# A graph layer on one core: node bias read from row 0 of the message buffers, y sums for a pair at once, second block scaled on VectorE

## The chip, the cores and the metric

The kernel runs on one core of a Trainium2 chip. A core has TensorE (PE in the profile, with its weight loads as PEld), VectorE (DVE), ScalarE (ACT), GpSimd (POOL), a queue engine SyncE (SP) and 16 DMA engines that all queues share. The metric is device time in microseconds (us), as a median of several runs.

## What is computed

The graph has 50,000 nodes and 25,000 edges sorted by `dst`, with rows of 128 numbers. Each edge's message is a normalised, gated product of its two end rows; messages with the same `dst` are averaged; each node is then updated from its own row and its mean message, and the result is normalised.

```python
em = jnp.concatenate([x[src], x[dst]], axis=-1)
em = jax.nn.relu(layer_norm(em @ msg_w + msg_b, msg_g, msg_beta)) * edge_weights[:, None]
msgs = jax.ops.segment_sum(em, dst, num_segments=num_nodes)
messages = msgs / (counts + 1e-08) * valid
gate = jax.nn.sigmoid(x @ gate_w + gate_b)
h_new = jax.nn.relu(layer_norm(jnp.concatenate([x, messages], -1) @ upd_w + upd_b, upd_g, upd_beta))
out = layernorm(x + gate * h_new + (1.0 - gate) * x)
```

## The kernel before, in words

Edges go in 49 groups of 512 (4 tiles of 128), nodes in 98 blocks of 512, two blocks to a pair, so 49 pairs. One step of the main loop handles one edge group and the parts of one pair, at different depths of the pipeline. Each engine has its own `step` function that lists its tasks by hand with a lag (how many steps the pair is behind the edge group) and a block number, 0 or 1. That list is the whole order; there is no scheduler. `walk` runs the steps, the middle ones in a loop.

An edge group: GpSimd gathers 8 tiles of rows of `x` (L466). PE transposes them, multiplies by the message weights into `ps_z` (L727, L729), on top of a bias matmul (L703). ACT squares, DVE scales (L1019), PE transposes back and multiplies (L742), DVE writes `msg_rows` (L1026), and SP stores them to the scratch table `rows_scratch` (L403). A row there is 129 numbers, 516 bytes: 128 values and the node's number.

A block of nodes: SP loads its `x_rows` (L366) and a **window** of the scratch table that holds all messages of the block: four tiles of 128 rows of 129, two to a DMA, the second DMA shifted by 64 rows (`load_window`, L384). The start row comes from a table, so each window DMA has its place in a register. DVE turns the node numbers in the window into a selection matrix `onehot` (`one_hots`, L1034). PE adds three products into `ps_u`: the bias (L703, bf16, one for two tiles), the node's own row (L761) and the selected messages (L763). ACT takes squares (L555), 1/deviation (L576, L581) and scales to `un` (L588), for both blocks. PE transposes (L778), ACT applies relu (L601), PE transposes back (L785), DVE forms `y` (L1048), its statistics (L1055), small sums of 4 numbers a partition (L1065 to L1085), ACT two small functions (L606, L611), DVE the output (L1100), and SP stores it (L399).

There are four window buffers, so SP may load a pair's two windows once the pair two before is through its updates (`pair_ready`); it must also wait until the next edge group's rows have landed in the scratch table (L376, L379), for the windows read them. All of SP's DMAs go through one queue, q1.

Of the kernel before, what the change touches and what calls it, by code (L numbers as in the profile page):

```python
# [6 lines left out]
ALU = mybir.AluOpType  # L7
# [13 lines left out]
FAR = float(1 << 20)  # L21
LN_EXP_SET = 6
# [28 lines left out]
def const_columns(wt):  # L51

    sizes = [P, T * P, 2 * T * P, 2 * T, 2, wt, 3, 1, T]
    return [sum(sizes[:i]) for i in range(len(sizes) + 1)]


def gnn_kernel(nc, x, src, dst, edge_weight, msg_w, msg_b, msg_g, msg_beta,  # L60
# [17 lines left out]
    C_IDENT, C_IOTA, C_BOUND, C_BOUNDC, C_TBASE, C_TILE, C_PART, C_LIMIT, C_WIN, C_END = const_columns(WT)  # L78

    with ExitStack() as ctx:  # L80
# [16 lines left out]
        iota_block = const_in[:, C_IOTA:C_IOTA + BN]  # L97
        tile_base = const_in[:, C_TILE:C_TILE + WT]
# [6 lines left out]
        msg_bias, upd_bias = sb("msg_bias", [P, T, P], BF16), sb("upd_bias", [P, 2, ROW], BF16)  # L105
        columns = sb("columns", [P, 4])
        gather_idx = sb("gather_idx", [P, EG, 2 * T], I32)
# [25 lines left out]
        gate_exp = [sb(f"gate_exp{s}", [P, T]) for s in range(2)]  # L133
        gate_small = [sb(f"gate_small{s}", [P, 3, T]) for s in range(2)]
        un = [sb(f"un{s}", [P, 512]) for s in range(2)]
        hT = [sb(f"hT{s}", [P, 512]) for s in range(2)]
        y = [sb(f"y{s}", [P, 512]) for s in range(2)]
        y_stats = [sb(f"y_stats{s}", [P, T, 6]) for s in range(2)]
        y_small = [sb(f"y_small{s}", [P, 6, T]) for s in range(2)]
        y_ln = [sb(f"y_ln{s}", [P, T]) for s in range(2)]  # L140
        y_rstd = [sb(f"y_rstd{s}", [P, T]) for s in range(2)]
# [23 lines left out]
        def u_tile(j, n):  # L165
# [3 lines left out]
            "p a (t h) -> p a t h", h=ROW)  # L169
        u_gates = u_by_bank[:, :, :, P:ROW]  # L170
# [3 lines left out]
        bias_in = sb("bias_in", [P, 2, ROW])  # L174
        bias_mean = sb("bias_mean", [P, 2])
        bias_left = sb("bias_left", [P, 3, 2, ROW])
        bias_part = sb("bias_part", [P, 3, 2, ROW], BF16)
        bias_sum = sb("bias_sum", [P, 3, 2, ROW])
# [109 lines left out]

        def all_edges(eng, task):
# [28 lines left out]
        def _(sp):  # L318
# [52 lines left out]
            def pair_ready(k):  # L371

                wait(sp, u_done, k.at(4, -4))
                if k.m is None:
                    for s in range(2):
                        sp.wait_ge(rows_stored[s], 16 * ((min(k.c + 2, EG) + 1 - s) // 2))  # L376
                else:
                    later = k.back(-1)
                    sp.wait_ge(rows_stored[later.c % 2], later.over(2).at(16, 16))  # L379

            def load_window(k, b, at):
# [25 lines left out]
            def step(at, by_window=True):  # L407
                node(load_x, at, 2, 1)
                node(store_out, at, 4, 0)
                edge(store_rows, at, 0)  # L410
                k = at.back(1)
                here = k.inside(0, NK)
                if here and by_window:
                    starts_at = [window_start(k, b) for b in range(2)]
                node(load_x, at, 1, 0)
                node(store_out, at, 4, 1)
                if here:
                    pair_ready(k)
                    for b in range(2):
                        if by_window:  # L420
                            load_window(k, b, starts_at[b])
                        else:
                            load_node_rows(k, b)
# [24 lines left out]
            with is_general(sp):  # L448
# [7 lines left out]
                walk(sp, lambda at: step(at, by_window=False), 4)  # L456
            with sp.Else():
                walk(sp, step, 4)
# [43 lines left out]
        def _(act):  # L502

            with nc.allow_non_contiguous_dma(reason="vectors of 128 as columns"):
# [5 lines left out]
                act.dma_start(bias_in[:, 1, P:ROW],  # L510
                              gate_b.rearrange("(h a) -> h a", a=1).to_broadcast([P, 1])).then_inc(loaded, 16)
                for i, v in enumerate((msg_b, upd_b)):
                    act.dma_start(bias_in[:, i, 0:P], v.rearrange("(a h) -> a h", a=1).to_broadcast([P, P])).then_inc(
# [52 lines left out]
            def gates(k, b):  # L566
                act.wait_ge(u_done, k.at(4, 2 * b + 2))
                if k.m is None:

                    wait(act, gate_chain, k.at(4, 2 * b - 3))  # L570
                nc.scalar.activation(gate_exp[b][:].rearrange("p (a t) -> p a t", a=2).unsqueeze(3), u_gates,
                                     ACT.Exp, scale=-1.0).then_inc(gate_exp_ready, 1)
# [31 lines left out]
            def y_ln_of(k, b):  # L604
                act.wait_ge(y_var_ready, k.at(2, b + 1))
                nc.scalar.activation(y_ln[b][:], y_small[b][:, 4], ACT.Ln, bias=LN_EPS / 4,  # L606
                                     scale=1.0 / P).then_inc(y_ln_ready, 1)

            def y_rstd_of(k, b):
                act.wait_ge(y_ln_ready, k.at(2, b + 1))  # L610
                nc.scalar.activation(y_rstd[b][:], y_ln[b][:], ACT.Exp, scale=-0.5).then_inc(y_rstd_ready, 1)  # L611
# [13 lines left out]
            def step(at):  # L625
                node(u_rstd_of, at, 4, 1)
                node(xT_of, at, 3, 0)
                node(first_norms, at, 4, 1)
                node(other_norms, at, 4, 1)
                edge(xsT_of, at, 0)  # L630
                edge(xdT_of, at, 0)
                node(first_squares, at, 3, 0)
                node(y_ln_of, at, 5, 1)
                node(hT_of, at, 4, 1)
                node(y_rstd_of, at, 5, 1)
                node(other_squares, at, 3, 0)
                node(xT_of, at, 3, 1)
                node(gates, at, 3, 0)
                node(u_ln_of, at, 3, 0)
                node(u_rstd_of, at, 3, 0)  # L640
                node(first_norms, at, 3, 0)
                node(other_norms, at, 3, 0)
                edge(z_squares, at, 0)
                node(y_ln_of, at, 4, 0)
                edge(z_ln_of, at, 0)
                node(y_rstd_of, at, 4, 0)
                edge(z_rstd_of, at, 0)
                node(hT_of, at, 3, 0)
                node(first_squares, at, 3, 1)
                node(other_squares, at, 3, 1)  # L650
                edge(emT_of, at, 0)
                node(u_ln_of, at, 3, 1)
                node(gates, at, 3, 1)
# [11 lines left out]
            walk(act, step, 5)  # L665

        @block.tensor
        def _(pe):
# [84 lines left out]
            def update(k, b, a):  # L753
# [5 lines left out]
                bias(ps_u[:, a * 512:a * 512 + 2 * ROW], upd_bias)  # L759
                for j in (2 * a, 2 * a + 1):  # L760
                    nc.tensor.matmul(u_tile(j, ROW), tile(xT[b], j), u_x_gate[:], start=False, stop=False,  # L761
# [55 lines left out]
            def step(at):  # L817
                node(back_transposes, at, 4, 0)
# [3 lines left out]
                node(first_update, at, 3, 0)  # L822
                node(update_transposes, at, 4, 1)
                node(other_update, at, 3, 0)
                node(x_transposes, at, 3, 1)
                edge(message, at, 0)
                node(back_transposes, at, 4, 1)
                node(first_update, at, 3, 1)
                node(update_transposes, at, 3, 0)
                node(other_update, at, 3, 1)  # L830
                node(x_transposes, at, 2, 0)
                edge(message_transposes, at, 0)
# [33 lines left out]
            walk(pe, step, 4, unroll=SLOTS)  # L866

        @block.vector
        def _(dve):
# [19 lines left out]
            v.memset(bias_in[:, 0, P:ROW], 0.0)  # L889
# [17 lines left out]
            v.tensor_reduce(bias_mean[:], bias_in[:, :, 0:P], AX.X, ALU.add)  # L907
# [3 lines left out]
            for i in range(2):  # L911
                v.tensor_scalar(bias_left[:, 0, i, 0:P], bias_in[:, i, 0:P], bias_mean[:, i:i + 1], None, ALU.add)
            v.tensor_copy(bias_left[:, 0, :, P:ROW], bias_in[:, :, P:ROW])
# [13 lines left out]
            for j in range(T):  # L927
                v.tensor_copy(msg_bias[:, j], bias_sum[:, 2, 0, 0:P])
            for j in range(2):
                last = v.tensor_copy(upd_bias[:, j], bias_sum[:, 2, 1])  # L930
            last.then_inc(params_ready, 1)
# [40 lines left out]
            def windows():  # L972
# [24 lines left out]
                link(v.tensor_scalar(ends[:], ends[:], float(P), block_start[:], ALU.subtract, ALU.is_gt))  # L997
# [31 lines left out]
            def one_hots(k, b):  # L1029
# [5 lines left out]
                                       tile_base[:, bass.ds(k.at(2 * T, b * T), 1)], tiles(iota_block),  # L1035
                                       ALU.subtract, ALU.is_equal).then_inc(hot_ready, 1)

            def residual(k, b):


                gates = gate_small[b]
                dve.wait_ge(gate_chain, k.at(4, 2 * b + 2))
                v.scalar_tensor_tensor(gates[:, 2], gates[:, 1], 2.0, gates[:, 1], ALU.add, ALU.mult).then_inc(
                    y_chain, 1)
                dve.wait_ge(h_back, k.at(2, b + 1))
                for j in range(T):
                    cols = slice(j * P, (j + 1) * P)
                    last = v.scalar_tensor_tensor(y[b][:, cols], ps_h[:, cols], gates[:, 1, j:j + 1],  # L1048
# [177 lines left out]
```

## Time and profile before

| | |
|---|---|
| median of 3 runs | 630.3 us (629.31 to 630.38) |
| the profiled execution | 628.39 us |
| its span on the core | 626.6 us |
| busy share of PE, DVE, ACT, GpSimd | 90%, 85%, 85%, 62% |
| mean granted TensorE clock | 0.97 of full speed |
| moved by DMA | 118.44 MB, 189 GB/s over the span |

The span has three parts: a setup to about 62 us, in which tables are built and the first groups run; 49 pairs of blocks in a loop of about 11 us each; and an end of some 25 us in which the last pair runs dry. A DMA queue's row in the profile gives packets (one for each contiguous row moved, and one of 4 bytes for each DMA engine's completion mark), the bytes, and the time of the packets as a share of 16 engines' time. One engine busy all the time is 1/16, or 6.3%. Packets on one engine overlap slightly, so a full engine reads a little above 100%.

### The profile page before, as it was taken

What the parts mean: (1) busy time and instruction counts of PE and PEld (TensorE: products, weight loads), DVE (VectorE), ACT (ScalarE), POOL (GpSimd) and SP (SyncE); (2) the same over time, 40 slices, a digit from 0 to 9 for tenths busy, and PEclk for the clock granted to TensorE, in tenths of its full rate; (3) what the DMA queues carried; (4) which work ended last, traced back from release to release, by engine and by line L of the source; (5) the groups of instructions that cost most, each with busy time, mean ns of one, the idle gap of its engine ahead of it and who ended that gap; (6) DMA issues with size and microseconds to landing.
All of it is one profiled execution on the core that took longest, in us unless ns stands there. A gap on an engine that the chain in (4) does not pass through costs nothing.

```text
span 626.6 us, 19668 instructions
## 1 busy us (share of the span) xinstructions
PE 563.5 (90%) x4796; PEld 541.1 (86%) x4796; DVE 529.8 (85%) x2428; ACT 535.7 (85%) x2500; POOL 387.1 (62%) x396
## 2 busy tenths in 40 slices
PE   1364799999999999999999999999999999999771
PEld 0343799999999999999999999999999999999761
DVE  3980158989989899998989989899899999989986
ACT  0021499999999999999999999999999999999883
POOL 1877777777777777777776767677676776300000
PEclk9976799999999999999999999999999999999996
DMA  4213577887878888787887877878787787756642
GB/s 112 64 48 88 136 200 206 208 234 202 231 215 216 221 209 225 204 221 217 217 230 189 226 213 208 230 195 221 210 214 219 204 229 197 208 156 171 182 117 67
DMA packets 199095, 118.44 MB, mean 189 GB/s; under 512 B 15053, under 2 KB 192662, under 8 KB 198934
## 3 DMA queue, kind: packets, MB, share of 16 engines
q1 hardware_dynamic: 184822, 91.95, 52.2%
q0 software_dynamic: 12544, 25.72, 17.2%
q10 hardware_dynamic: 1696, 0.40, 0.3%
q8 instruction: 13, 0.21, 0.1%
q14 instruction: 20, 0.16, 0.1%
HBM read 79.04 MB, written 38.97 MB: 188 GB/s over the span
## 4 chain that ended last, share of the span: by engine, by line
PE 87%; DVE 5%; ACT 5%; issue 2%; DMA 1%; SPq 0%; DVEq 0%; ACTq 0%
PE ps_u L761 14%; PE ps_u L763 13%; PE ps_z L742 9%; PE ps_z L729 7%; PE ps_z L727 7%; PE ps_t L778 7%; PE ps_x L750 6%; PE ps_h L785 6%; PE ps_u L703 3%; PE ps_xs L710 3%; PE ps_xs L736 3%; PE ps_xd L710 3%; PE ps_z L703 2%; DMA halo_i<-in_dst 1%; ACT squares L555 1%
## 5 line engine op out<-in xcount | busy, mean ns | idle before, releaser
L466 POOL DMA_INDIRECT pair_rows<-in_x,gather_idx x392 | 386.9, 987 | 151.5 <-issue 112.9
L761 PE MATMUL ps_u<-u_x_gate,xT 128*128 128x129 f32 x784 | 151.7, 275 | 0.0
L763 PE MATMUL ps_u<-window,onehot 128*128 128x128 f32 x784 | 151.2, 274 | 0.0
L761 PEld LDWEIGHTS ps_u<-u_x_gate,xT 128*128 128x128 f32 x784 | 118.7, 191 | 1.6
L763 PEld LDWEIGHTS ps_u<-window,onehot 128*128 128x128 f32 x784 | 119.0, 192 | 0.0
L588 ACT ACTIVATE un<-ps_u,u_rstd 128x128 f32<-128x128 f32 x392 | 112.0, 372 | 3.2
L1100 DVE TENSOR_SCALAR out_rows<-y,y_small,y_rstd 128x128 f32<-128x128 f32 x392 | 110.5, 355 | 4.6 <-ACT y_rstd L611 4.6
L1048 DVE SCALAR_TENSOR_TENSOR y<-ps_h,gate_small,x_rows 128x128 f32<-128x128 f32 x392 | 109.8, 342 | 1.2 <-PE ps_h L785 1.2
L555 ACT ACTIVATE squares<-ps_u 128x128 f32<-128x128 f32 x392 | 105.7, 288 | 3.0 <-PE ps_u L763 2.9
L555 ACT ACTIVATION_READ_ACCUMULATOR squares<-ps_u 128x1 f32 x392 | 85.6, 219 | 0.0
L1055 DVE BATCH_NORM_STATS2 y_stats<-y 128x6 f32<-128x128 f32 x392 | 84.6, 278 | 0.0
L601 ACT ACTIVATE hT<-ps_t,columns 128x512 f32<-128x512 f32 x98 | 78.4, 800 | 6.7 <-PE ps_t L778 2.9
L729 PE MATMUL ps_z<-weights,xdT 128*128 128x128 f32 x392 | 77.4, 280 | 0.0
L727 PE MATMUL ps_z<-weights,xsT 128*128 128x128 f32 x392 | 77.4, 280 | 0.0
L1034 DVE SCALAR_TENSOR_TENSOR onehot<-window,const_in 128x512 f32<-128x512 f32 x98 | 72.6, 741 | 1.8 <-DMA window<-rows_scratch 1.6
L1026 DVE TENSOR_TENSOR msg_rows<-ps_z,weight_col 128x512 f32<-128x512 f32 x49 | 33.9, 692 | 42.3 <-PE ps_z L742 42.3
L727 PEld LDWEIGHTS ps_z<-weights,xsT 128*128 128x128 f32 x392 | 65.0, 196 | 1.9
L519 ACT COPY xsT<-ps_xs 128x512 f32<-128x512 f32 x49 | 29.7, 607 | 40.9 <-PE ps_xs L710 40.9
L529 ACT ACTIVATE squares<-ps_z 128x128 f32<-128x128 f32 x196 | 52.2, 304 | 11.2 <-PE ps_z L729 11.2
L729 PEld LDWEIGHTS ps_z<-weights,xdT 128*128 128x128 f32 x392 | 61.2, 197 | 0.0
L742 PEld LDWEIGHTS ps_z<-weights,emT 128*128 128x128 f32 x392 | 49.3, 197 | 13.8 <-ACT emT L544 13.8
L742 PE MATMUL ps_z<-weights,emT 128*128 128x128 f32 x392 | 58.9, 295 | 2.2 <-ACT emT L544 2.2
(133 smaller groups left out, 1119.2 us busy)
## 6 DMA issues: line engine op xcount, KB each, us to landing
window<-rows_scratch SPq DMA_DIRECT2D x196, 129.0 KB
x_rows<-in_x SPq DMA_DIRECT2D x98, 256.0 KB
out<-out_rows SPq DMA_DIRECT2D x98, 256.0 KB
rows_scratch<-msg_rows SPq DMA_DIRECT2D x49, 258.0 KB, 3.1
pair_rows<-in_x,gather_idx POOLq DMA_INDIRECT x392
const_in<-in_constants SPq DMA_DIRECT2D x1, 1037.0 KB, 5.1
rows_scratch<-pad_rows SPq DMA_DIRECT2D x5, 64.5 KB, 2.7
weights<-in_L_gnn_msg_w ACTq DMA_DIRECT2D x1, 128.0 KB, 5.3
```

The lines of the kernel that those rows point to most:

```text
L466: return nc.gpsimd.indirect_dma_start(rows[:, j * P:(j + 1) * P], None, x, bass.IndirectOffsetOnAxis(ap=offsets, axis=0))
L555: last = nc.scalar.activation(squares[:, b, j * P:(j + 1) * P], u_tile(j, P), ACT.Square, accum_out=u_square[b][:, j:j + 1])
L588: last = nc.scalar.activation(un[b][:, j * P:(j + 1) * P], u_tile(j, P), ACT.Copy, scale=u_rstd[b][:, j:j + 1])
L601: nc.scalar.activation(hT[b][:], ps_t[:], ACT.Relu, bias=columns[:, 3:4], scale=columns[:, 2:3]).then_inc(hT_ready, 1)
L727: nc.tensor.matmul(tile(ps_z, j), tile(xsT[g.c % 2], j), w_src, start=False, stop=False, skip_group_check=True)
L729: last = nc.tensor.matmul(tile(ps_z, j), tile(xdT[g.c % 2], j), w_dst, start=False, stop=True, skip_group_check=True)
L742: last = nc.tensor.matmul(tile(ps_z, j), tile(emT[g.c % 2], j), u_msg, start=True, stop=True)
L761: nc.tensor.matmul(u_tile(j, ROW), tile(xT[b], j), u_x_gate[:], start=False, stop=False, skip_group_check=True)
L763: last = nc.tensor.matmul(u_tile(j, P), tile(onehot[b], j), window[slot][:, j * ROW:j * ROW + P], start=False, stop=True, skip_group_check ...
L1048: last = v.scalar_tensor_tensor(y[b][:, cols], ps_h[:, cols], gates[:, 1, j:j + 1], x_rows[2 * (k.c % 2) + b][:, cols], ALU.mult, ALU.add)
L1055: last = v.bn_stats(y_stats[b][:, j], y[b][:, j * P:(j + 1) * P])
L1100: last = v.tensor_scalar(out_rows[b][:, cols], y[b][:, cols], y_small[b][:, 5, j:j + 1], y_rstd[b][:, j:j + 1], ALU.subtract, ALU.mult)
```

## The change

- **Bias of the update.** The bias matmuls into `ps_u` go. Instead row 0 (partition 0) of each window buffer holds the bias, written once in the setup, with a node number `ALWAYS`, and `iota_block` has `ALWAYS` in its row 0 too, so that the selection matrix picks it for every node. The window DMAs therefore write partitions 1 to 127 only: 127 rows for each tile and not 128. The bias of the gate goes into ScalarE's `Exp`.
- **Small sums.** The gate's and y's small sums are made for both blocks of a pair at once (8 numbers a partition), and so are ScalarE's two small functions on y. `y` has four buffers.
- **Scaling.** `un` of block 1 is made by VectorE in one instruction (`u_norms`), that of block 0 still by ScalarE in four.
- **Orders.** All `step` lists are new, one pair deeper. SP loads the windows of a pair apart: block 1 right behind two output stores, block 0 behind the store of the edge group's rows.

```diff
+            def window_free(k, b):
+                wait(sp, u_done, k.at(4, 2 * b - 6))
+                if b == 1:
+                    return
...
             def load_window(k, b, at):
                 slot = 2 * (k.c % 2) + b
                 for i in range(2):
-                    sp.dma_start(window[slot][:].rearrange("p (a i h) -> p i a h", i=2, h=ROW)[:, i],
+                    sp.dma_start(window[slot][1:P, :].rearrange("p (a i h) -> p i a h", i=2, h=ROW)[:, i],
                                  rows_dram[bass.ds(at + i * HALF, 2 * P), :].rearrange(
-                                     "(a p) h -> p a h", p=P)).then_inc(win_loaded[slot], 16)
+                                     "(a p) h -> p a h", p=P)[0:P - 1]).then_inc(win_loaded[slot], 16)
...
             def step(at, by_window=True):
+                node(store_out, at, 5, 0)
+                node(store_out, at, 5, 1)
+                if b.inside(0, NK):
+                    load_messages(b, 1, at_b)
                 node(load_x, at, 2, 1)
-                node(store_out, at, 4, 0)
                 edge(store_rows, at, 0)
+                if a.inside(0, NK):
+                    load_messages(a, 0, at_a)
                 node(load_x, at, 1, 0)
...
                 wait(pe, un_ready, k.at(4, 2 * b - 1 + a))
-                bias(ps_u[:, a * 512:a * 512 + 2 * ROW], upd_bias)
...
+            def u_norms(k, b):
+                dve.wait_ge(u_rstd_ready, k.at(2, b + 1))
+                dve.wait_ge(gate_exp_ready, k.at(2, b + 1))
+                wait(dve, un_in, k.at(2, b - 1))
+                v.tensor_tensor(un[b][:].rearrange("p (a t h) -> p a t h", a=2, h=P), u_values,
+                                u_rstd[b][:].rearrange("p (a t) -> p a t", a=2).unsqueeze(3).to_broadcast(
+                                    [P, 2, 2, P]), ALU.mult).then_inc(un_ready, 2)
...
+                node(residual, at, 4, 0)
+                edge(z_norm, at, 0)
+                node(result, at, 5, 0)
+                node(result, at, 5, 1)
                 node(residual, at, 4, 1)
+                edge(rows, at, 0)
+                node(one_hots, at, 2, 0)
+                node(y_halves, at, 4, 0)
                 node(y_halves, at, 4, 1)
+                pair(y_sums, at, 4)
                 node(one_hots, at, 2, 1)
+                node(u_norms, at, 3, 1)
+                pair(gate_sums, at, 3)
```

SP's queue in the loop, before: one step's output store, the four window DMAs of a pair (128 partitions, 2 tiles, 129 numbers), and a load of `x_rows`.

```order
L399 DMA out<-out_rows 128x4x128
L262 REGISTER_ALU
L384 ISA
L384 DMA window<-rows_scratch 128x2x129
L384 ISA
L384 DMA window<-rows_scratch 128x2x129
L384 ISA
L384 DMA window<-rows_scratch 128x2x129
L384 ISA
L384 DMA window<-rows_scratch 128x2x129
```

The edge rows' store (L403) stands further up in the same step, with a load and an output store between it and the four.

The same queue in the changed kernel, in the loop: the two output stores, then the window DMAs of block 1, now with 127 partitions.

```order
L415 REGISTER_ALU
L418 ISA
L418 DMA out<-out_rows 128x4x128
L418 ISA
L418 DMA out<-out_rows 128x4x128
L267 REGISTER_ALU
L403 ISA
L403 DMA window<-rows_scratch 127x2x129
L403 ISA
L403 DMA window<-rows_scratch 127x2x129
```

What follows it there: `x_rows`, the edge rows' store, and block 0's window DMAs, of which the first is shown.

```order
L267 REGISTER_ALU
L376 ISA
L376 DMA x_rows<-in_x 128x4x128
L379 ISA
L379 TENSOR_LOAD start_row
L379 ISA x2
L421 REGISTER_ALU
L422 ISA
L422 DMA rows_scratch<-msg_rows 128x4x129
L267 REGISTER_ALU
L403 ISA
L403 DMA window<-rows_scratch 127x2x129
```

The four window DMAs stood in one row and now stand in two pairs, the second right behind the store that it has to wait for.

PE, first update of block 0 in the loop, before:

```order
L703 MATMUL ps_u<-upd_bias,ones_bf 128x258
L761 MATMUL ps_u<-u_x_gate,xT 128x129
L763 MATMUL ps_u<-window,onehot 128x128
L761 MATMUL ps_u<-u_x_gate,xT 128x129
L763 MATMUL ps_u<-window,onehot 128x128
L775 REGISTER_ALU
L778 MATMUL ps_t<-const_in,un 128x128 x4
```

and in the changed kernel, without the bias:

```order
L774 MATMUL ps_u<-u_x_gate,xT 128x129
L776 MATMUL ps_u<-window,onehot 128x128
L774 MATMUL ps_u<-u_x_gate,xT 128x129
L776 MATMUL ps_u<-window,onehot 128x128
L788 REGISTER_ALU
L267 REGISTER_ALU
L791 MATMUL ps_t<-const_in,un 128x128 x4
```

Four such bias matmuls go in each step. In the setup of both kernels SP also issues loads of 128, 67 and 1 rows of the edge arrays, one behind the other, `weight_f` last. SP's queue before:

```order
L330 DMA weight_f<-in_edge_weight 128x128
L331 DMA weight_f<-in_edge_weight 67x128
L332 DMA weight_f<-in_edge_weight 1x40
L353 DMA rows_scratch<-pad_rows 128x129 x5
L403 DMA rows_scratch<-msg_rows 128x4x129 x2
```

These rows are of before; in the changed kernel they stand in the same order.

## Rows read from the trace of the kernel before

**Rows 1.** Page, part 1: busy time and share of each engine

```profile
PE 563.5 (90%) x4796; PEld 541.1 (86%) x4796; DVE 529.8 (85%) x2428; ACT 535.7 (85%) x2500; POOL 387.1 (62%) x396
```

**Rows 2.** Busy us by stretch (three loop steps), clock, DMA share, GB/s

```profile
200.79:212.01 11.22, 11.22 (x101) 10.90 (x100) 10.19 (x50) 11.05 (x53) 8.48 (x10) 1.00 0.82 220
212.01:222.98 10.97, 10.97 (x99) 10.63 (x98) 10.05 (x48) 10.63 (x51) 8.53 (x9) 1.00 0.80 206
222.98:234.23 11.25, 11.25 (x101) 10.93 (x100) 10.23 (x50) 11.09 (x53) 8.51 (x10) 1.00 0.84 228
```

**Rows 3.** The chain that ended last, in order of time, inside a step

```profile
207.06 0.11 PE ps_u L703
```

**Rows 4.** SP's queue in order of time, one step: start, us

```profile
200.79 2.12 SPq L384 DMA_DIRECT2D window<-rows_scratch  x4
...
207.81 0.40 SPq L403 DMA_DIRECT2D rows_scratch<-msg_rows  x1
...
212.01 2.15 SPq L384 DMA_DIRECT2D window<-rows_scratch  x4
```

**Rows 5.** Page, part 3: DMA queues, packets, MB, share of 16 engines

```profile
q1 hardware_dynamic: 184822, 91.95, 52.2%
q0 software_dynamic: 12544, 25.72, 17.2%
```

**Rows 6.** Page, part 6: DMA issues, KB each, us to landing

```profile
window<-rows_scratch SPq DMA_DIRECT2D x196, 129.0 KB
x_rows<-in_x SPq DMA_DIRECT2D x98, 256.0 KB
out<-out_rows SPq DMA_DIRECT2D x98, 256.0 KB
rows_scratch<-msg_rows SPq DMA_DIRECT2D x49, 258.0 KB, 3.1
```

**Rows 7.** SP's queue in the setup: 67-row loads, and one of 128

```profile
2.14 0.59 SPq L331 DMA_DIRECT2D src_i<-in_src  x1
...
3.77 0.28 SPq L331 DMA_DIRECT2D halo_i<-in_dst  x1
...
12.86 0.35 SPq L330 DMA_DIRECT2D weight_f<-in_edge_weight  x1
13.25 0.28 SPq L331 DMA_DIRECT2D weight_f<-in_edge_weight  x1
```

**Rows 8.** DMA packets from 13.8 to 14.3 us, the 128-row load

```profile
DMA packets 145, 0.07 MB, mean 132 GB/s; under 512 B 16, under 2 KB 145, under 8 KB 145
```

**Rows 9.** DMA packets from 14.35 to 16.35 us, the 67-row load

```profile
q0 software_dynamic: 30, 0.06, 10.4%
q1 hardware_dynamic: 69, 0.03, 6.8%
```

**Rows 10.** DMA packets from 7.55 to 9.75 us, two 67-row loads queued

```profile
q1 hardware_dynamic: 85, 0.04, 6.3%
```

**Rows 11.** DMA packets from 11.1 to 11.93 us, a load of 127 short rows

```profile
GB/s 6 5 5 5 3 5 5 5 5 5 5 5 5 5 5 5 5 5 5 5 5 3 5 5 5 5 5 5 5 5 5 5 5 5 5 5 5 5 3 4
DMA packets 119, 0.00 MB, mean 5 GB/s; under 512 B 119, under 2 KB 119, under 8 KB 119
```

**Rows 12.** DMA packets from 12.7 to 12.97 us, 128 short rows

```profile
q1 hardware_dynamic: 143, 0.00, 33.5%
```

**Rows 13.** DMA packets from 242.5 to 243 us, window rows alone

```profile
q1 hardware_dynamic: 326, 0.17, 113.9%
```

**Rows 14.** SP's queue: first window loads, and the last

```profile
62.70 2.12 SPq L384 DMA_DIRECT2D window<-rows_scratch  x4
...
598.59 2.10 SPq L384 DMA_DIRECT2D window<-rows_scratch  x4
```

**Rows 15.** Groups by line, shapes apart: busy us, mean ns, idle before

```profile
L588 ACT ACTIVATE un<-ps_u,u_rstd 128x128 f32<-128x128 f32 x392 | 112.0, 372 | 3.2
L606 ACT ACTIVATE y_ln<-y_small 128x4 f32<-128x4 f32 x98 | 24.5, 250 | 6.3 <-DVE y_small L1085 6.2
L1019 DVE TENSOR_TENSOR zn<-ps_z,z_rstd 128x512 f32<-128x512 f32 x49 | 33.6, 687 | 25.5 <-ACT z_rstd L539 24.8
```

More of the change, by code:

```diff
@@ L21 @@
 FAR = float(1 << 20)
+ALWAYS = float(1 << 60)
 LN_EXP_SET = 6
@@ L132, in gnn_kernel @@
         u_rstd = [sb(f"u_rstd{s}", [P, T]) for s in range(2)]
-        gate_exp = [sb(f"gate_exp{s}", [P, T]) for s in range(2)]
-        gate_small = [sb(f"gate_small{s}", [P, 3, T]) for s in range(2)]
+        gate_exp = [sb(f"gate_exp{s}", [P, 2, T]) for s in range(2)]
+        gate_small = sb("gate_small", [P, 3, 2 * T])
         un = [sb(f"un{s}", [P, 512]) for s in range(2)]
         hT = [sb(f"hT{s}", [P, 512]) for s in range(2)]
[L137 to L141, printed above, removed]
+        y = [sb(f"y{s}", [P, 512]) for s in range(4)]
+        y_stats = sb("y_stats", [P, 2 * T, 6])
+        y_small = sb("y_small", [P, 6, 2 * T])
+        y_ln = sb("y_ln", [P, 2 * T])
+        y_rstd = sb("y_rstd", [P, 2 * T])
         out_rows = [sb(f"out_rows{s}", [P, 512]) for s in range(2)]
@@ L287, in node, with pair @@
                 task(k, b)
+        def pair(task, at, lag):
+            k = at.back(lag)
+            if k.inside(0, NK):
+                task(k)
         def all_edges(eng, task):
@@ L379, in pair_ready, with load_messages @@
                     sp.wait_ge(rows_stored[later.c % 2], later.over(2).at(16, 16))
+            def load_messages(k, b, at):
+                window_free(k, b)
+                if at is None:
+                    load_node_rows(k, b)
+                else:
+                    load_window(k, b, at)
             def load_window(k, b, at):
@@ L407, in step @@
             def step(at, by_window=True):
+                b, at_b = at.back(2), None
+                if by_window and b.inside(0, NK):
+                    at_b = window_start(b, 1)
+                node(store_out, at, 5, 0)
+                node(store_out, at, 5, 1)
+                if b.inside(0, NK):
+                    load_messages(b, 1, at_b)
                 node(load_x, at, 2, 1)
-                node(store_out, at, 4, 0)
+                a, at_a = at.back(1), None
+                if by_window and a.inside(0, NK):
+                    at_a = window_start(a, 0)
                 edge(store_rows, at, 0)
[L411 to L414, printed above, removed]
+                if a.inside(0, NK):
+                    load_messages(a, 0, at_a)
                 node(load_x, at, 1, 0)
[L416 to L423, printed above, removed]
             def sum_by_node():
@@ L625, in step @@
             def step(at):
[L626 to L629, printed above, removed]
+                node(u_rstd_of, at, 5, 1)
+                pair(y_rstd_of, at, 6)
+                edge(z_squares, at, 1)
+                edge(z_ln_of, at, 1)
+                edge(z_rstd_of, at, 1)
+                node(first_squares, at, 4, 0)
+                node(hT_of, at, 5, 1)
+                node(other_squares, at, 4, 0)
+                edge(emT_of, at, 1)
+                node(u_ln_of, at, 4, 0)
+                node(gates, at, 4, 0)
+                node(u_rstd_of, at, 4, 0)
+                node(xT_of, at, 4, 1)
+                node(first_norms, at, 4, 0)
+                node(other_norms, at, 4, 0)
                 edge(xsT_of, at, 0)
                 edge(xdT_of, at, 0)
[L632 to L653, printed above, removed]
+                node(hT_of, at, 4, 0)
+                node(first_squares, at, 4, 1)
+                node(other_squares, at, 4, 1)
+                node(xT_of, at, 3, 0)
+                node(u_ln_of, at, 4, 1)
+                node(gates, at, 4, 1)
+                pair(y_ln_of, at, 5)
             act.add_instruction(mybir.InstLoadActFuncSet(
@@ L664, in _ @@
                 head()
-            walk(act, step, 5)
+            walk(act, step, 6)
         @block.tensor
@@ L888, in _ @@
             v.memset(count_side[1][:], 0.0)
-            v.memset(bias_in[:, 0, P:ROW], 0.0)
+            for s in range(4):
+                v.memset(window[s][0:1, :].rearrange("p (j h) -> p j h", h=ROW)[:, :, P:ROW], ALWAYS)
             dve.wait_ge(pads_ready, 4)
@@ L926, in _ @@
                                             ALU.mult, ALU.add))
[L927 to L931, printed above, removed]
+            v.tensor_copy(msg_bias[:], bias_sum[:, 2].unsqueeze(1).to_broadcast([P, T, P])).then_inc(params_ready, 1)
             dve.wait_ge(edges_loaded, 16 * 12)
@@ L1118, in step @@
             def step(at):
+                node(residual, at, 4, 0)
+                edge(z_norm, at, 0)
+                node(result, at, 5, 0)
+                node(result, at, 5, 1)
                 node(residual, at, 4, 1)
[L1120 to L1121 removed]
+                edge(rows, at, 0)
+                node(one_hots, at, 2, 0)
+                node(y_halves, at, 4, 0)
                 node(y_halves, at, 4, 1)
[L1123 to L1126 removed]
+                pair(y_sums, at, 4)
                 node(one_hots, at, 2, 1)
[L1128 to L1130 removed]
+                node(u_norms, at, 3, 1)
+                pair(gate_sums, at, 3)
             def sum_by_node():
                 v.memset(xT[0][:], 0.0).then_inc(zeros_ready, 1)
+                for j in range(T):
+                    last = v.tensor_scalar(iota_block[0:1, j * P:(j + 1) * P], iota_row[0:1, :], float(j * P), None,
+                                           ALU.add)
+                link(last)
                 for j in range(T):
@@ L1174, in _ @@
                 head()
-            walk(dve, step, 4)
+            walk(dve, step, 5)
 def constants(n_nodes):
```

200 lines of the change are left out of this document (97 added, 103 removed).

## The prediction

> **What bounds the kernel now.** I read the busy shares first, then three steps of the loop, then the chain, then SP's queue. PE is busiest over the span [rows 1]. Inside the loop a step takes 10.97 to 11.25 us, 11.15 in the mean, and PE is busy in all of it, ACT in 10.92 and DVE in 10.16 [rows 2]. The chain stays on PE there, a bias matmul into `ps_u` costing it 0.11 us [rows 3]. So PE sets the step, ACT is 0.2 us behind it and DVE 1.0. The DMA engines are no bound, but they are not idle either: 0.80 to 0.84 of 16 engines [rows 2]. That last figure is a mean over 16 engines, and it says nothing about one of them. This matters here, because the change alters the shape of the most numerous transfer.
>
> **The part that decides: window loads of 127 partitions.** A window DMA carried 128 x 2 rows of 516 bytes and now carries 127 x 2. The bytes hardly change. How the rows spread over the DMA engines may. The trace has a pair of loads that shows it, issued 0.4 us apart (12.86 and 13.25) with rows of 512 bytes [rows 7]. The load of 128 rows gives 145 packets in the half microsecond from 13.8: 16 of 4 bytes, the completion marks of 16 engines, and 129 of 512, the load's own and one that follows [rows 8]. The load of 67 rows takes the stretch from 14.35 to 16.35: q1 has 69 packets in 2.0 us and they fill 6.8% of 16 engines, which is one engine, full [rows 9]. Half the rows took four times as long. GpSimd's gathers share that stretch (q0) but on their own account, and they start in its second half.
>
> 127 itself occurs too, with rows of 36 bytes: 119 packets come at an even 5 GB/s through the whole 0.83 us, one after another [rows 11], at the rate of one engine. The load of 128 such rows, with what is around it, has 143 packets in 0.27 us at 33.5% of 16 engines, or 5.4 engines at once [rows 12]. So 67 and 127 partitions go to one engine, 128 go to 16. Is it the same engine each time? Two loads of 67 rows, issued at 2.14 and 3.77 [rows 7], neither has ended at 7.55, and from there to 9.75 q1 never has more than one engine: 85 packets at 6.3% of 16, exactly 1/16 [rows 10]. Had they gone to different engines, it would read 12.5%. So all 196 window DMAs of the changed kernel should go to one engine, the same for all, one behind the other.
>
> What that engine has to do for a pair of blocks:
>
> 1. Window rows: 4 DMAs x 127 x 2 = 1016 rows. The best pace that the trace has for these very rows is 326 packets in 0.5 us on 16 engines [rows 13], 16 x 500 / 326 = 24.5 ns a row on each. The slow end is the 67-row load, 2.0 us / 69 = 29 ns a packet [rows 9]. I take 27 ns, between them: 1016 x 27 = 27.4 us (24.9 to 29.5). Before, the same engine had 1024 / 16 = 64 of these rows, 1.7 us.
> 2. Its share of everything else. `x_rows` and `out` are two issues a pair of 256 KB, `rows_scratch` one of 258 KB [rows 6], together 2 x 512 + 2 x 512 + 512 = 2560 rows, 160 on each engine, at 25 ns 4.0 us. Gathers: 17.2% of the span on each engine [rows 5], 107.8 / 49 = 2.2 us a pair, inflated by the queueing among full engines that will now be absent; I take 1.5. Together 5.5 us (4.7 to 7.1; the upper end is 52.2% + 17.2% of 626.6 us over 49 pairs, 8.9, less the 1.8 of the windows before).
> 3. A pause in each step. SP issues block 0's windows only once the store of the edge rows has landed (`window_free`, L391 of the changed kernel), and that store is now queued right behind block 1's 508 rows on the same engine; the order shows the two next to each other. From issue to landing a store takes 3.1 us when little is ahead of it [rows 6]. About 1.1 of that is before its first packet, as with the 67-row load (issued 13.25, packets from 14.35) [rows 7, 9]; about 0.9 is its rows; so some 1.2 us lie between its last packet and the landing, and the next window DMA needs its own 1.1 before its first packet. The engine stands idle for 2.3 us (0 to 4: gathers may fill it, and SP may be late).
>
> Sum: 27.4 + 5.5 + 2.3 = 35.2 us a pair, where a step takes 11.15 now. Is the pause the only one? Once block 1's window lands, DVE has a selection matrix, `u_norms`, gate sums, residual, `zn` and eight output instructions before SP can store the outputs and issue the next pair of windows: about 7 us, and block 0's 508 rows take the engine 13.7. So the next DMAs are in the queue in time, and the engine runs dry once a step, not twice. POOL's gathers are four groups ahead. The clock of TensorE, 1.00 in the loop now [rows 2], may fall while PE waits; PE's 11 us could double and would still be covered by 35.
>
> **The parts that would pay.** Four bias matmuls a step at 0.11 us go from PE [rows 3]: 0.44 us, PE 10.7. From ACT go four scalings of `un`, 4 x 372 ns = 1.5 us by busy time (they overlap, so some 1.1), and one of two `y_ln` and `y_rstd`, 0.25 us and about as much [rows 15]: ACT 9.4. DVE takes one instruction on 128x512 out of PSUM, which by `zn` is 0.69 us [rows 15], and loses half of 18 small ones, which I put at as much again, 0.7: DVE stays at 10.2. The setup trades a few short instructions for others, within 1.5 us either way. All of it lies beside a DMA engine that needs 35 us a step, so in the forecast it is worth nothing; it is the whole of the second rival.
>
> **The sum.** First windows are issued at 62.7 us, as before [rows 14]. 49 pairs x 35.2 = 1725. Behind the last window's issue the kernel runs dry: 626.6 - 600.7 = 26 us before [rows 14], of which 2 are the window's own landing, counted already: 24. Span 62.7 + 1725 + 24 = 1812, and 1.8 us lie around the span (628.39 - 626.6). The profiled execution is 1.9 us under the median shown, so 1814 to 1816: **1815 us**. With the low ends of all terms, 49 x 29.6 + 87 = 1540; with the high ones, 49 x 40.6 + 87 + 2 = 2080.
>
> **The rivals.**
>
> *Two engines.* The window's load has 127 x 2 rows, and the rows above are of flat loads. If the spread went by a number that the factor 2 enters, two engines would share the rows: 13.7 + 5.5 + 2.3 = 21.5 us a pair, 49 x 21.5 + 89 = 1143 us. For it: no row shows a prime count with a second dimension. Against: a load of 128 x 2 and one of 128 read alike. The Trainium skill, "DMA: Bandwidth & Descriptors", section "Why a DMA increments its semaphore by 16 and not by 1", says that the number of engines is the largest up to 16 that divides the slowest dimension of both sides, so that 127 partitions give 1 whatever stands behind; by it this rival is out and the sum stands at 1815. The 128- and 67-row loads agree with it; no run here shows it for three dimensions. I leave 3 in 100.
>
> *All 16 engines, and the change pays.* It needs the window DMAs of the loop, whose place comes from a register, to be spread otherwise than the setup's fixed ones. Then PE's 0.44 us a step goes: 49 x 0.44 = 22 us, 630 - 22 = 608 us, 595 to 620 with the waits that ACT frees (PE's bias waits for `un`). This is the side "not slower". It decides if q1's share shows no engine ahead of the others. 5 in 100.
>
> *All 16 engines, and a new wait.* Block 1's window is now used by DVE in the step in which it is issued: between lie a residual, `rows`, a selection matrix, eight statistics and six sums, about 5 us, and two window DMAs take 1.06 us to issue [rows 4] and, by the store, 3.1 to land [rows 6]. If landing slips by 2 us, DVE's 10.2 becomes 12.2, over 11.15: 49 x 1 = 50 us, 680. It decides from a slip of 1 us. 1 in 100.
>
> *Nothing seen*, within 1.3 us of 630: 1 in 100.
>
> **How the numbers follow.** The forecast has 90 in 100, and its range is that of its unknown terms, pulled in a little since they won't all fall on one side: 1560 to 2060. Slower by over 0.2%: 0.90 + 0.03 + 0.01 = 0.94. Within 0.2%, about what a measurement of this kernel can tell from no change: 0.01. Faster: 0.05.
>
> **What the profile after would show.** DMA share falls from 0.8 to about (35.2 + 15 x 5.5) / 16 / 35.2 = 0.2; PE's busy share falls to about a third; SP waits on `rows_scratch` landings in every step, where now it hardly does; DVE's selection matrices (L1047) wait for the window DMAs, up to some 14 us each, 98 times. POOL waits for PE. A step repeats every 35 us. Wrong would be the forecast if the DMA share stays at 0.8, or if the step lands near 21 us (two engines). If the step is 30 or 40, a term is off: the first if the engine is full throughout, the third if it has holes.

## The result and the profile after

The changed kernel takes **1752.9 us** (1749.6 to 1753.8), the kernel before 629.8 us: a ratio of 2.782 (2.777 to 2.787). The range was 1560 to 2060, the forecast 1815.

The profiled execution took 1753.8 us with a span of 1752.0. Its busy line against [rows 1], from the page of the changed kernel:

```profile
PE 773.7 (44%) x4600; PEld 726.2 (41%) x4600; DVE 542.8 (31%) x2038; ACT 508.7 (29%) x2206; POOL 379.7 (22%) x396
DMA  2321322222232222223222222222222222212212
```

No engine that computes is busy half the time, and the DMA engines are at two tenths in their mean. PE is at 44% and not at the third that was expected: over the step from 828.99 to 863.00 us its granted clock is 0.70 and it is busy for 15.4 us. A mean of 0.2 hides the one that is full. The packets of one window load, from 834 to 844 us, show it:

```profile
GB/s 21 21 19 21 19 19 23 17 19 21 19 19 21 19 19 19 19 21 19 19 19 21 19 19 19 19 21 19 19 21 19 19 19 21 19 19 19 19 21 19
q1 hardware_dynamic: 365, 0.19, 7.5%
```

The rows come at an even 19 GB/s. 365 packets in 10 us is one every 27.4 ns, and 7.5% of 16 engines is 1.2 engines' worth: one engine, whose packets overlap a little (the same overlap lets 16 engines read 113.9% in [rows 13]). The pace isn't quite steady: 215 packets from 817 to 823 us are one every 27.9 ns, 183 from 870.5 to 875 one every 24.6.

SP's queue in order of time over one step (start, us), against [rows 4]:

```profile
828.99 7.86 SPq L403 DMA_DIRECT2D window<-rows_scratch  x2
837.11 6.60 SPq L376 DMA_DIRECT2D x_rows<-in_x  x1
844.83 0.42 SPq L422 DMA_DIRECT2D rows_scratch<-msg_rows  x1
849.15 4.98 SPq L403 DMA_DIRECT2D window<-rows_scratch  x2
854.39 6.28 SPq L376 DMA_DIRECT2D x_rows<-in_x  x1
861.74 1.01 SPq L418 DMA_DIRECT2D out<-out_rows  x2
863.00 7.67 SPq L403 DMA_DIRECT2D window<-rows_scratch  x2
```

A step is 863.00 - 828.99 = 34.0 us. Two things stand here. SP waits 4 us between the store at 844.83 and the next windows at 849.15. In that wait the slow engine has its pause, the third term of the forecast; from 848.4 to 850.7 us, 2.3 us, the DMA view has three packets in all:

```profile
q1 hardware_dynamic: 3, 0.00, 1.7%
```

And two window issues, or one of `x_rows`, take 5 to 8 us, where they took 1.1 and 0.4: more on that at the end. The waits of the engines that compute, the two longest in total (us, times, longest):

```profile
DVE onehot L1047 <- DMA window<-rows_scratch: 1033.3, 98, 16.3
POOL pair_rows L484 <- PE ps_xs L724: 984.4, 41, 27.1
```

The selection matrix waits for its window all 98 times.

### The profile page after: what moved, and what is told of

The parts are those of the page before. It is cut to its first block, busy times and chain, and to the rows that moved or that the text cites. A ratio compares the mean times of both kernels' runs of the same rounds, so it can differ in the third digit from the quotient of the medians.

```text
span 1752.0 us, 18557 instructions
## 1 busy us (share of the span) xinstructions
PE 773.7 (44%) x4600; PEld 726.2 (41%) x4600; DVE 542.8 (31%) x2038; ACT 508.7 (29%) x2206; POOL 379.7 (22%) x396
## 4 chain that ended last, share of the span: by engine, by line
SPq 71%; DMA 17%; issue 5%; PE 4%; DVE 3%; ACT 1%; DVEq 0%; ACTq 0%
SPq L376 33%; SPq L403 31%; DMA rows_scratch<-msg_rows 9%; DMA window<-rows_scratch 8%; SPq L379 3%; SPq L418 3%; PE ps_u L774 1%; PE ps_u L776 1%; DVE y L1077 0%; PE ps_t L791 0%; DMA halo_i<-in_dst 0%; DVE un L1055 0%; SPq L422 0%; SPq L267 0%; DVE out_rows L1113 0%
## 5 line engine op out<-in xcount | busy, mean ns | idle before, releaser
L774 PE MATMUL ps_u<-u_x_gate,xT 128*128 128x129 f32 x784 | 207.1, 355 | 571.3 <-DVE un L1055 566.8
L774 PEld LDWEIGHTS ps_u<-u_x_gate,xT 128*128 128x128 f32 x784 | 161.6, 256 | 585.8 <-DVE un L1055 480.6
L764 PE MATMUL ps_x<-const_in,x_rows 128*128 128x128 f32 x392 | 91.7, 379 | 348.0 <-DMA x_rows<-in_x 348.0
L764 PEld LDWEIGHTS ps_x<-const_in,x_rows 128*128 128x128 f32 x392 | 66.7, 199 | 357.6 <-DMA x_rows<-in_x 357.6
L776 PEld LDWEIGHTS ps_u<-window,onehot 128*128 128x128 f32 x784 | 162.2, 256 | 0.0
L568 ACT COPY xT<-ps_x 128x512 f32<-128x512 f32 x98 | 57.3, 585 | 347.2 <-PE ps_x L764 347.2
L741 PE MATMUL ps_z<-weights,xsT 128*128 128x128 f32 x392 | 119.3, 406 | 0.0
L741 PEld LDWEIGHTS ps_z<-weights,xsT 128*128 128x128 f32 x392 | 109.9, 324 | 7.2
L791 PE MATMUL ps_t<-const_in,un 128*128 128x128 f32 x392 | 81.0, 345 | 1.7 <-DVE un L1055 1.7
L791 PEld LDWEIGHTS ps_t<-const_in,un 128*128 128x128 f32 x392 | 65.3, 185 | 2.0 <-DVE un L1055 2.0
```

Of the source, the lines that this page charges most:

```text
L741: nc.tensor.matmul(tile(ps_z, j), tile(xsT[g.c % 2], j), w_src, start=False, stop=False, skip_group_check=True)
L764: last = nc.tensor.transpose(tile(ps_x, j), tile(x_rows[slot], j), ident)
L776: last = nc.tensor.matmul(u_tile(j, P), tile(onehot[b], j), window[slot][:, j * ROW:j * ROW + P], start=False, stop=True, skip_group_check ...
L791: last = nc.tensor.transpose(tile(ps_t, j), tile(un[b], j), ident)
```

## The experiments

In this section "a step" is the mean distance between two starts of the instruction that writes `msg_rows`, from the fourth group to the last, in the profiled execution. For the kernel before these are 84.62 and 583.84 us, 45 steps of 11.09; for the changed kernel 105.63 and 1638.10, 45 steps of 34.06. The two of the changed kernel:

```profile
105.63 0.69 DVE L1039 TENSOR_TENSOR msg_rows<-ps_z,weight_col 128x512 f32<-128x512 f32 x1 [4.34 <-PE ps_z L756]
1638.10 0.69 DVE L1039 TENSOR_TENSOR msg_rows<-ps_z,weight_col 128x512 f32<-128x512 f32 x1 [0.46 <-PE ps_z L756]
```

**One edit undone, one edit done.** The first kernel is the changed one with windows of 128 partitions again. It leaves out the update's bias, for the windows overwrite row 0; every instruction stays:

```
-                    sp.dma_start(window[slot][1:P, :].rearrange(
+                    sp.dma_start(window[slot][:].rearrange(
...
-                                     "(a p) h -> p a h", p=P)[0:P - 1])
+                                     "(a p) h -> p a h", p=P))
```

> The changed kernel with one thing undone: the window DMAs write 128 partitions again (the bias row is overwritten, so the update's bias is left out; every instruction stays). Theory, one DMA engine for 127 partitions: the DMA share in the loop goes back to about 0.8, a step is set by PE at 11.15 - 0.44 = 10.7 us, time 595 to 620, about 608. Rival, the new orders or the pause behind the store carry part of the 1123 us: it stays above 700. Rival, a new wait of VectorE on the window it uses in the step of its issue: 640 to 700, with waits on the window DMAs before the selection matrices.

Measured: 636.2 us, ratio 1.012 (1.008 to 1.015), which lies in none of the three ranges, between the theory's 620 and the last rival's 640. The 1117 us between this and the changed kernel are all of the one partition. But the remaining change isn't worth 22 us, as I had said; it costs 7. That is taken up below.

The second is the kernel before with only this done to it (`window[slot][1:P, :]`, source rows `[1:P]`, and row 0 set once). It leaves out the messages that stand in row 0 of a window:

> The kernel before with one thing done: its window DMAs leave out partition 0 and carry 127 x 2 rows (what stands in row 0 of a window is left out of the sums). Theory: the same slowdown from that alone, in this order all four window DMAs stand in one row and the store of the edge rows is ahead of them, so 28.3 us of rows and 5.5 of the rest a pair, and a pause of 0 to 2.3: 34 to 36 us a pair, 1690 to 1850. Rival, it takes the new orders as well: under 1200.

Measured: 1759.5 us in one run, with a step of 34.2 us. The old orders slow down just as the new ones do. Its SP queue:

```profile
817.93 19.49 SPq L384 DMA_DIRECT2D window<-rows_scratch  x4
```

where four issues took 2.12 us before [rows 4].

**The same rows, cut otherwise.** This kernel computes the whole result and loads the same 127 rows of a window with as many DMAs; they are cut by partitions where the changed kernel cuts by tiles:

```
-                for i in range(2):
-                    sp.dma_start(window[slot][1:P, :]....[:, i], ...)
+                rows = rows_dram[bass.ds(at, SPAN), :]
+                for low, high in ((1, 113), (113, P)):
+                    part = rows[low - 1:high - 1]
+                    sp.dma_start(window[slot][low:high, :].rearrange("p (j h) -> p j h", h=ROW),
+                                 bass.AP(tensor=part.tensor, offset=part.offset,
+                                         ap=[[ROW, high - low], [HALF * ROW, T], [1, ROW]],
+                                         runtime_checks=part.runtime_checks)).then_inc(win_loaded[slot], 16)
```

> The changed kernel, whole, with the same 127 rows of a window loaded by two DMAs that are cut by partitions, not by tiles: partitions 1 to 112 (112 = 16 x 7) and 113 to 127 (15), four tiles each. Theory: 16 and 15 engines, so about 32 rows on each engine and a window: as e1_after_128, 595 to 620, and faster than the kernel before by 2 to 5%. Rival, a start at partition 1 is what confines a DMA to one engine: over 1500. If the small DMA goes to few engines: 620 to 700.

Measured: 642.7 us, ratio 1.020 (1.017 to 1.024). The start at partition 1 is not the cause, the count is. The time missed the theory as that of the first kernel did. It lies in the range given for a small DMA on few engines, but so does the first kernel's 636.2, so this range decides nothing; the cut itself can have cost at most the 6.5 us between the two.

**How many engines for which count.** Two kernels load 124 and 122 partitions of each window and leave the last rows out, one run each.

> The changed kernel with 124 partitions loaded (1 to 124; rows 125 to 127 of each window hold no messages, which leaves those out). 124 = 4 x 31. Theory, the engines used are the largest number up to 16 that divides the partitions: 4 engines with 248 rows a pair each, 6.9 us at 27.8 ns, 5.7 of the rest: 12.6 us a step, 49 x 12.6 + 87 = 704 (650 to 730). Rival, any count that isn't a multiple of 16 goes to one engine: 1740. Rival, only odd counts do: about 640.

> The changed kernel with 122 partitions loaded (rows 123 to 127 of each window left out). 122 = 2 x 61. Theory: 2 engines with 488 rows a pair each, 13.6 us at 27.8 ns, and 5.7: 19.3 us a step, 49 x 19.3 + 87 = 1030 (970 to 1080). Rivals as for 124: 1740, or about 640.

Measured: 771.6 and 1065.3 us. Neither rival is near: counts that aren't multiples of 16 can go to several engines, and even counts are slow too. With 2 engines the time is inside what was expected; with 4 it is 42 us over its upper end. First and last start of `msg_rows` in the two, 124 first:

```profile
84.57 0.69 DVE L1042 TENSOR_TENSOR msg_rows<-ps_z,weight_col 128x512 f32<-128x512 f32 x1 [2.77 <-PE ps_z L756]
711.75 0.69 DVE L1042 TENSOR_TENSOR msg_rows<-ps_z,weight_col 128x512 f32<-128x512 f32 x1 [0.31 <-PE ps_z L756]
```

```profile
87.43 0.69 DVE L1042 TENSOR_TENSOR msg_rows<-ps_z,weight_col 128x512 f32<-128x512 f32 x1 [3.88 <-PE ps_z L756]
991.29 0.69 DVE L1042 TENSOR_TENSOR msg_rows<-ps_z,weight_col 128x512 f32<-128x512 f32 x1 [0.47 <-PE ps_z L756]
```

| partitions | engines by the largest divisor up to 16 | rows on each, a pair | us at 27.4 ns | step, us | what is left, us |
|---|---|---|---|---|---|
| 127 | 1 | 1016 | 27.8 | 34.06 | 6.2 |
| 122 | 2 | 488 | 13.4 | 20.09 | 6.7 |
| 124 | 4 | 248 | 6.8 | 13.94 | 7.1 |

The rows on each engine explain the three steps up to a rest of 6.2 to 7.1 us. I had counted on 5.7; with four engines 1.4 us a step, 69 us in all, are more. How exact the rest is hangs on the pace: one and the same count ran at 24.6 to 27.9 ns a row.

The trace doesn't number the engines, but it shows how many work where the window rows move alone. First 122 partitions, from 407.5 to 409.5 us, then 124, from 662 to 662.9:

```profile
q1 hardware_dynamic: 164, 0.08, 14.2%
q1 hardware_dynamic: 147, 0.08, 28.4%
```

127 partitions read 19 GB/s and 7.5% above. These are 42 and 84 GB/s, and 1.9 and 3.8 times the share: two engines and four, each at the quicker pace of the one (24.4 and 24.5 ns a row). The Trainium skill, "DMA: Bandwidth & Descriptors", section "Why a DMA increments its semaphore by 16 and not by 1", gives this rule for the slowest dimension of both sides, and the three runs agree with it for windows with a second dimension.

**Why the rest of the change doesn't pay.** The expectation was that PE, freed of four bias matmuls, sets the step at 10.7 us. First the bias matmuls alone, out of the kernel before (in `update` the line `bias(ps_u...)` goes and the next matmul starts the bank):

> The kernel before without the four bias matmuls into ps_u a step (the bias is left out). By the chain's 0.11 us each: 49 x 0.44 = 22 us less, 608. Rival, ACT is 0.2 us behind PE and takes over as the bound: only 49 x 0.23 = 11 us or less, 617 to 625.

Measured: 617.6 us, ratio 0.981 (0.978 to 0.984): 11 to 12 us, and not 22. The number is the rival's, ScalarE close behind. PE still reads as full, and ScalarE nearly so. Busy us from 300 to 400 us (span, PE, PEld, DVE, ACT, POOL, clock, DMA share, GB/s):

```profile
300.00:400.00 100.00, 99.95 (x860) 95.83 (x859) 93.36 (x432) 98.89 (x472) 73.56 (x77) 1.00 0.82 223
```

A busy PE isn't PE at its peak: its step is 10.84 us here, four matmuls of 0.11 us shorter would be 10.65. That ScalarE holds it back is the likely reason and isn't shown by itself; the trace's waits name it only 6 times, 8.2 us in all, from 100 to 600 us.

In the first kernel (changed, 128 partitions) I took VectorE for what fills. Its queue has hardly a gap from one selection matrix of block 1 to the next:

```profile
301.55 0.75 DVE L1047 SCALAR_TENSOR_TENSOR onehot<-window,const_in 128x512 f32<-128x512 f32 x1
302.24 0.69 DVE L1055 TENSOR_TENSOR un<-ps_u,u_rstd 128x512 f32<-128x512 f32 x1
...
308.60 0.69 DVE L1039 TENSOR_TENSOR msg_rows<-ps_z,weight_col 128x512 f32<-128x512 f32 x1 [0.25 <-PE ps_z L756]
...
312.40 0.75 DVE L1047 SCALAR_TENSOR_TENSOR onehot<-window,const_in 128x512 f32<-128x512 f32 x1
```

That is 10.85 us with 0.25 us of waiting. But 10.85 is the length of the step, not VectorE's work in it. Busy us of the engines over the same stretch (order as above):

```profile
301.55:312.40 10.85, 10.78 (x94) 10.30 (x93) 10.40 (x39) 9.81 (x46) 7.68 (x9) 1.00 0.79 216
```

PE is the fuller of the two, 10.78 against 10.40, and the chain through this step is all PE but for one `emT` of ScalarE, 0.79 us; VectorE isn't on it. Over a longer stretch VectorE does come in: from 100 to 600 us PE is idle for 16.7 us, where it was for 5.2 before, and 11.0 of them are waits for the scaling `un` of block 1, which VectorE now makes. The next runs went after VectorE's fullness. First I moved that scaling back to ScalarE (`first_norms` and `other_norms` at the head of its step, no `u_norms`; this kernel too leaves the update's bias out):

> e1_after_128 with the scaling of block 1 back on ScalarE, at the head of its step, and no scaling on VectorE (bias left out as there). Theory, VectorE with 10.9 us of 11.1 a step is what bounds e1: it is freed of 0.69 us, ScalarE takes 1.1 and stands at 10.9: 620 to 632, faster than e1 (636). Rival, the new place of the window loads behind the output stores holds e1 back: within 3 us of e1's 636, with the waits on windows as before.

Measured: 634.4 us, ratio 1.007 (1.004 to 1.009). The number lies outside the theory and within the rival's 3 us, but the rival's waits on windows didn't stay as before: they rose from 16.0 to 25.7 us. VectorE falls to 85 to 88% busy, but ScalarE rises to 94 to 97%, so one nearly full engine was exchanged for another. Next, the place of the window loads:

```
+                if b.inside(0, NK):
+                    load_messages(b, 1, at_b)
                 node(store_out, at, 5, 0)
                 node(store_out, at, 5, 1)
-                if b.inside(0, NK):
-                    load_messages(b, 1, at_b)
```

> e1_after_128 (636.2 us) with SP issuing block 1's window ahead of the two output stores and not behind them. Theory, what is left of e1's loss is that VectorE uses this window in the step in which it is issued, about 4 us after: the waits on the window (16.0 us from 100 to 600 us) and PE's on the scaling behind them (11.0 and 15.7) go, 615 to 628. Rival, VectorE's own 10.9 us of work a step holds e1: within 4 us of 636.

> e3_split (the whole change, windows cut at partition 113, 642.7 us) with the same move. Theory: 618 to 632, so no slower than the kernel before; it would have to come under 622 to beat the bias row alone in the old orders. Rival: within 4 us of 643.

> e7_after_124 (771.6 us where 704 was expected; rows 125 to 127 of the windows left out) with the same move. Theory, its step of 13.9 us was set by the ring result, output store, window load, selection matrix, not by the four engines' 12.6: 690 to 740. Rival, the four engines are full, and a row costs more than 27.8 ns: within 10 us of 771.

Measured: 640.1 us (ratio 1.016, 1.014 to 1.019; without the update's bias), 648.0 us (ratio 1.029, 1.025 to 1.032) and 770.4 us (one run). None is faster, so the theory that the late window load holds the new orders back falls. The first and the third are the rival's; the second is 5 us slower than its 643, outside both. In the first of the three the waits on the window are down and those of PE on VectorE are not, here from 100 to 600 us, first with the loads behind the stores, then ahead of them:

```profile
DVE onehot L1047 <- DMA window<-rows_scratch: 16.0, 25, 1.6
...
PE ps_u L774 <- DVE un L1055: 11.0, 15, 2.1
```

```profile
PE ps_u L774 <- DVE un L1055: 13.5, 23, 1.9
...
DVE onehot L1047 <- DMA window<-rows_scratch: 8.9, 15, 1.4
```

Idle time was taken from VectorE and it gave nothing. The last kernel takes work from VectorE and gives it to nobody: the scaling covers 4 columns of 128, so most of block 1's update is left out.

```
-                v.tensor_tensor(un[b][:].rearrange(...), u_values, ...
+                v.tensor_tensor(un[b][:].rearrange(...)[:, :, :, 0:4], u_values[:, :, :, 0:4], ...
```

> e1_after_128 (636.2 us) with VectorE's scaling of block 1 cut from 128 to 4 columns a tile, all waits kept (most of block 1's update is left out). It frees VectorE of 0.5 to 0.6 us a step and gives nothing to ScalarE. Theory, after the order of the window loads fell as a cause: VectorE's work without a gap, 10.85 us a step, is the floor of e1, with PE's 10.7 just below: the shortest steps fall to 10.7 and the mean of 11.17 by 0.2 to 0.5, 612 to 628. Rival, the steps over 10.9 come from late transfers or PE's order and don't depend on how full VectorE is: 630 to 636.

Measured: 627.3 us, ratio 0.995 (0.993 to 0.998), 9 us under the first kernel, at the slow edge of what the theory expected. The step falls from 11.17 to 11.01 us, 0.16 and not the 0.2 to 0.5 expected; 25 of the 45 steps lie between 10.65 and 10.85 us where 4 did. So VectorE's scaling is a part of it, not all. Whether it counts by filling VectorE or by handing block 1 to PE late, this run doesn't separate, for it changes both.

The other part is the end. From the last `msg_rows` to the end of the span:

| kernel | step | last `msg_rows` | span | the end |
|---|---|---|---|---|
| before | 11.09 | 583.84 | 626.6 | 42.8 |
| changed, 128 partitions | 11.17 | 584.91 | 634.0 | 49.1 |
| the same, scaling of 4 columns | 11.01 | 580.02 | 626.8 | 46.8 |

The two rows of the changed kernel with 128 partitions:

```profile
82.33 0.69 DVE L1039 TENSOR_TENSOR msg_rows<-ps_z,weight_col 128x512 f32<-128x512 f32 x1 [2.77 <-PE ps_z L756]
...
584.91 0.69 DVE L1039 TENSOR_TENSOR msg_rows<-ps_z,weight_col 128x512 f32<-128x512 f32 x1 [0.30 <-PE ps_z L756]
```

Of its 7.4 us over the kernel before, 6.3 come after the last edge group. The new orders run deeper: behind its last `msg_rows` VectorE has six selection matrices to make, five before, and a block in this end takes about 5 us (`un` of block 1 at 589.74, 599.78 and 609.80, two blocks apart each). That one block more is drained with no edge group beside it. I hadn't counted it.

**A version that beats both.** The bias in row 0 of the windows, taken alone into the kernel before, with its orders, its sums and its scaling, and windows cut at partition 113. It computes the whole result.

> The kernel before, its orders, its sums and its scaling on ScalarE, with the first part of the change alone (bias in row 0 of the window buffers, no bias matmuls), the windows loaded by two DMAs of 112 and 15 partitions. Theory, the bias matmuls are what the change had to give and 127 partitions what it cost: as the kernel without the bias, ratio 0.981, plus what the cut costs (e3 against e1: up to 6 us): 616 to 624, faster than before, correct output. Rival, the cut DMAs cost more where all are issued in one row: 628 or more.

Measured: **622.3 us**, ratio 0.988 (0.986 to 0.990). Of the 11 to 12 us that the bias matmuls cost, 7 are left; its step is (577.61 - 85.91) / 45 = 10.93 us, beside 10.84 without any bias.

## Where the prediction was right and where not

- **The bound before** (PE 11.15, ACT 10.92 a step): right. With ACT 0.2 us behind, the bias matmuls alone give 11 us and not 22; the number fits, the cause isn't shown apart.
- **127 partitions go to one DMA engine, the same for all loads**: right. The time moves by 1117 us with this edit and by 1130 us the other way in the kernel before, and where the window rows move alone the DMA view shows one engine's rate. It was read from small loads of the setup that cost nothing there.
- **Term 3, the pause, 2.3 us**: right in the step shown, 848.4 to 850.7 us. Its parts came from the landing of a store in the kernel before and a 67-row load of the setup, so to meet it to a tenth is in part luck.
- **Terms 1 and 2, the window rows and the engine's other rows, 27.4 + 5.5 = 32.9 us**: too large together. 34.06 - 2.3 = 31.8 us. By 27.4 ns a row the windows are 27.8 us and the rest 4.0; by 24.6 ns they are 25.0 and the rest 6.8. Which of the two was too large the paces of 24.6 to 27.9 ns leave open.
- This is where the 62 us between 1815 and 1753 went: 49 x 1.1 = 56 us of them.
- **All the rest is covered by the slow engine**: right for this kernel.
- **The rival in which all engines are used and the change pays, 608 us**: wrong in its price, as the kernel with 128 partitions showed (636). PE's 0.44 us a step do not come off in full even in the old orders (0.25 there). In the new orders two things stood at nothing in the sum: PE's waits for the scaling that VectorE now makes, 11.0 us from 100 to 600 us, and the drain of a deeper pipeline, 6.3 us. The work of the other engines was put too low, but by little. VectorE is busy for 462.0 of those 500 us, 10.3 us a step and not 10.2, and ScalarE for 442.4, 9.9 and not 9.4.
- **The rival with a new wait on the window**: the wait is there with 128 partitions, 16.0 us in 500, but to halve it (8.9) gained nothing.

Open: steps of the new orders scatter between 10.8 and 12 us, also where VectorE has room, and no run names what makes the long ones. Nor is it known whether the rest of a step really grows to 7.1 us with 4 engines: at the 24.5 ns of the 0.9 us shown above, the 248 rows take 6.1 us and 7.9 are left, with 2 engines at 24.4 ns 8.2, and with one at 24.6 ns 9.1, pause included.

## What to carry to other kernels

Before you trim one partition off a DMA, ask how many engines the new count gets: 128 to 127 cost a factor of 2.8 and the mean DMA share didn't warn, it fell. If a row has to stay untouched, cut the load into counts that divide well (112 and 15) with the number of DMAs unchanged; here that cost 5 to 7 us against 128 partitions. And when two engines stand within 2% of each other, price a saving on the first by the distance to the second, and add what a deeper pipeline costs at its end.

## What the runs showed of the hardware that I had not expected

An issue on SP's queue grows with the backlog of a single DMA engine. Before, a load of `x_rows` occupied SP for 0.4 us; in the changed kernel, with one engine behind and fifteen nearly idle, it took 6 to 7 us, and with 122 partitions, two engines, 3.0 to 3.6 (400 to 425 us). That the full engine is what holds the issue is read from these times and not shown apart. The chain that ended last runs through these issues:

```profile
SPq L376 33%; SPq L403 31%; DMA rows_scratch<-msg_rows 9%; DMA window<-rows_scratch 8%; SPq L379 3%; SPq L418 3%; PE ps_u L774 1%; PE ps_u L776 1%; DVE y L1077 0%; PE ps_t L791 0%; DMA halo_i<-in_dst 0%; DVE un L1055 0%; SPq L422 0%; SPq L267 0%; DVE out_rows L1113 0%
```

So the chain names SP's instructions, 64% of the span, where the cause is an engine that the page has no row for. In the kernel before with 127 partitions the four window issues of a step took 19.5 us instead of 2.1. I saw no cost of it in the sum: the slow engine's pause in the step shown ends behind the store's landing, not behind a long issue.
